# A gather loop of a graph network: one wait of GpSimd per superstep in place of four

## The chip, the cores and the metric

The kernel runs on one core of a Trainium2 chip. The metric is the device time of one execution in microseconds (us). The engines are TensorE (PE in the profile; its weight loads are PEld), VectorE (DVE), ScalarE (ACT), GpSimd (POOL, Pool in the text) and SyncE (SP), which here only sends transfers. Each runs its own list of instructions and meets the others at semaphores.

## The reference, cut to what matters

A graph of 12500 nodes with 64 features and 200000 edges, sorted by their target node `dst`, passes through two layers. The first is the one that matters here:

```
all_feat = concat([x[dst], x[src], edge_attr, u_per_node[dst]], axis=-1)
msg = relu(all_feat @ W1 + b1)
agg = segment_sum(msg, dst, num_segments=x.shape[0])
x = layernorm(x + relu(concat([x, agg, u_per_node]) @ W2 + b2))
```

The second layer is an attention over the same edges (a score, a softmax over the edges of a target, and a weighted sum), and ends in a layernorm too.

## The kernel before, in words

The kernel is one program with stages one after the other: inputs and the table of products `Btab` = x W1b, one row of 64 numbers per node; the first loop (`phase_layer0`); the nodes between the layers (`phase_mid`); the second loop (`phase_layer1`); the end. The change touches the first loop alone, though its helper `gathers` serves both.

*Tiles and slots.* The edges form 1563 tiles of 128. A tile whose targets lie in more than one block of 128 nodes is worked on once for each of these blocks; with these repeats there are 1664 slots, 8 of which (`O`) make a step: 208 steps (`SO`). The gathers go by supersteps of 8 tiles without repeats, 196 of them. A step thus uses tiles of its own superstep or of one up to 13 (`BEHIND`) earlier, the more so the further the loop has come.

*The ring.* Pool fetches, for each tile, the rows of `Btab` of its 128 source nodes with an indirect transfer into one of the 184 places of `ring` (23 supersteps, `RT`). This is line 453 in `gathers`. The loop needs these rows when VectorE fills `full` (line 853), which adds the ring's rows to TensorE's products of the edge features. A place may be overwritten when the step that last read it has filled: for gather j = 0 of superstep s Pool waits, at line 449, on `used`, which is S["full"] in the first loop, until the fill of step s - 10 has been made. At lines 451 and 452 it waits again, ahead of gathers j = 2, 4 and 6, on `summed`, which is S["acc"], until VectorE has made 2, 4 or 6 sums (line 846) of the tiles of step s - 11; VectorE makes those in step s - 9, behind the fill of that step. After its gather j = 3 Pool tells (`landed`) that the superstep before has arrived, once it has.

*One step s of the loop, by engine.* VectorE: one-hots of step s + 1 (line 830, float32, which waits for S["s"], the sums' products of an older step; and line 834, bf16); two reduces (line 873) of TensorE's products into `p_t`, which wait for S["m0"] and S["m1"]; loads of registers; the fill (line 853), which waits for `landed`; then, by turns, 8 sums of step s - 2 into the nodes' rows (line 846, on S["acc"]) and 8 additions to `p_t` (line 859). ScalarE: the relu of `p_t` into `msg` (line 632). TensorE: for step s + 1, behind the fill of s, 8 matmuls of line 719 and 4 of line 724 (float32, 2 passes each), which give S["m0"] after half of them and S["m1"] after all; then, behind the relu, the 8 matmuls of line 732 (float32, 16 passes) that give S["s"]. SP: the edge features of a later step (line 565) and, every 4 steps, the targets' rows `drow` (line 465).

Of the kernel before, what the change touches and what calls it, by code (L numbers as in the profile page):

```python
# [22 lines left out]
O = 8  # L23
# [6 lines left out]
RT = 23  # L30
# [45 lines left out]
CHUNKS = [(q, q + QC) for q in range(0, NQ, QC)]  # L76
# [353 lines left out]
def place(t):  # L430

    return t % RING


def gathers(e, A, ring, table, idx, s_g, landed, used, summed, free={}):

    tiles = lambda s: min(NT - s * O, O)


    def counted(s):  # L440
        e.wait_ge(s_g[s % len(s_g)], 16 * sum(tiles(i) for i in range(s % len(s_g), s + 1, len(s_g))))
        e.sem_inc(landed, 1)

    for t in range(NT):
        s, j = divmod(t, O)
        if s in free and j == 0:
            e.wait_ge(*free[s])
        if s >= RT and j == 0:
            e.wait_ge(used, s - RT + BEHIND + 1)

        if s >= RT and j in (2, 4, 6):
            e.wait_ge(summed, O * (s - RT + BEHIND - 1) + j)
        e.indirect_dma_start(out=ring[:, place(t), :], out_offset=None, in_=table[:, :],  # L453
                             in_offset=bass.IndirectOffsetOnAxis(ap=idx[:, t:t + 1], axis=0)).then_inc(s_g[s % len(s_g)], 16)
        if s and j == min(3, NT - s * O - 1):
            counted(s - 1)
    counted(TO - 1)
# [11 lines left out]
def phase_layer0(nc, A):  # L469
# [3 lines left out]
    with ExitStack() as ctx:  # L473
# [3 lines left out]
        ring = sb("ring0", [P, RING, D], F32)  # L477
# [3 lines left out]
        idx = A.idx0  # L481
# [5 lines left out]
        full = sb("full", [P, 2 * O, D], F32)  # L487

        XT0 = RING - NB
# [31 lines left out]
        S = {n: sem("l0_" + n) for n in names}  # L521
        s_g = [sem(f"l0_g{q}") for q in range(4)]
# [3 lines left out]
        T = {n: sem("t_" + n) for n in ("dve count before middle low high typ val sq sel tab d0 rows rowt rowi table dh dl lt yt ys "  # L526
                                        "drow typd ix a hi lo rem parts zero").split()}
# [44 lines left out]

        @block.gpsimd
        def _(e):
            gathers(e, A, ring, A.Btab, idx, s_g, S["landed"], S["full"], S["acc"], {XT0 // O: (T["a"], len(CHUNKS))})

        @block.scalar
        def _(e):
# [648 lines left out]
def phase_layer1(nc, A):  # L1227

    QO, QT, QV = 7, 5, 4
    with ExitStack() as ctx:  # L1230
# [43 lines left out]
        @block.gpsimd  # L1274
        def _(e):
            gathers(e, A, ring, A.Ztab, idx, s_g, S["landed"], S["s"], S["acc"])
# [425 lines left out]
```

## Time and profile before

| what | us |
|---|---|
| median of 3 runs | 5584.88 (5583.66 to 5586.26) |
| the profiled execution | 5585.71 |
| its span, from the first instruction to the last | 5584.0 |
| busy in it: PE, DVE, POOL, ACT | 3080.6, 2980.1, 3034.1, 1278.0 |
| first loop, from its first reduce to its last steps | about 178 to 2850 |

The rows below are of that one execution, in microseconds from the span's start. In a timeline row stand the start, the duration, the engine, the line, the operation, what it writes and reads, how many were merged, and in brackets the idle time of the engine before it with what ended it. "remote" is an end that the profile can't pin to an instruction, "issue" is time in which nothing was waited for that the profile shows. The ends of matmuls are modelled. A gather's row (DMA_INDIRECT) covers Pool's own work on it, not the transfer.

### The profile page before, as it was taken

The page shows a single profiled execution, that of the slowest core. Times are in us where ns is not written, and L with a number is a line of the kernel's source. Part 1 is how long each engine was busy: PE and PEld are TensorE (multiplying, and loading weights), DVE is VectorE, ACT ScalarE, POOL GpSimd, SP SyncE. Part 2 cuts the span into 40 slices and gives each one's busy share as a digit, 9 for nine tenths or more (in the row PEclk, how much of TensorE's full clock was granted, in tenths as well). Part 3 has the DMA queues.
Part 4 walks back from the last instruction along what each step waited for, and adds up shares of the span by engine and source line. Part 5 has one row for each costly group of instructions (what it writes and reads, how often), then busy time and mean ns, then how long its engine had stood idle before and what let it go on. Part 6 is the DMA issues. An engine that isn't in the chain of part 4 may idle for free. (4 is left out here: it accounts for less than half of the span.)

```text
span 5584.0 us, 71029 instructions
## 1 busy us (share of the span) xinstructions
PE 3080.6 (55%) x17849; PEld 2768.8 (50%) x17849; DVE 2980.1 (53%) x9486; ACT 1278.0 (23%) x4180; POOL 3034.1 (54%) x3265
## 2 busy tenths in 40 slices
PE   2265555455555555545784066555555656655576
PEld 1264444444444444444772055555555555555565
DVE  1265554455555555555773065555555555555567
ACT  0100000000000000000022044444444444444455
POOL 5525555555555555555215706666666666666631
PEclk5555555555555555555566555555555555555555
DMA  3211111111111111111125101111111111111111
GB/s 115 82 45 51 46 53 53 45 51 46 54 52 45 52 46 53 52 44 52 53 100 181 28 27 46 47 47 47 47 47 47 47 47 47 47 47 47 47 38 32
DMA packets 172540, 300.15 MB, mean 54 GB/s; under 512 B 71719, under 2 KB 78235, under 8 KB 158844
## 3 DMA queue, kind: packets, MB, share of 16 engines
q0 software_dynamic: 100032, 105.03, 9.8%
q1 hardware_dynamic: 70662, 188.25, 9.4%
q8 instruction: 173, 2.83, 0.2%
q10 hardware_dynamic: 1462, 2.30, 0.1%
q14 instruction: 211, 1.73, 0.1%
HBM read 260.36 MB, written 34.99 MB: 53 GB/s over the span
## 5 line engine op out<-in xcount | busy, mean ns | idle before, releaser
L453 POOL DMA_INDIRECT ring<-Btab,idx x1563 | 1486.5, 951 | 1214.7 <-DVE XA L846 610.3
L453 POOL DMA_INDIRECT ring<-Ztab,idx x1563 | 1479.9, 947 | 922.2 <-issue 400.0
L719 PE MATMUL p_m<-A,oht 128*128 x1664 | 438.3, 365 | 1061.8 <-DVE full L853 1023.5
L1344 PE MATMUL p_s<-ring,ohx 128*128 x3328 | 808.9, 420 | 191.2 <-issue 187.2
L732 PE MATMUL p_s<-msg,oh 128*128 128x64 f32 x3328 | 763.8, 418 | 178.2 <-issue 137.0
L1344 PEld LDWEIGHTS p_s<-ring,ohx 128*128 128x128 f32 x3328 | 738.8, 325 | 214.4 <-issue 214.1
L732 PEld LDWEIGHTS p_s<-msg,oh 128*128 128x128 f32 x3328 | 731.0, 329 | 204.8 <-issue 204.5
L873 DVE TENSOR_REDUCE p_t<-p_m 128x256 f32<-128x768 f32 x416 | 380.0, 958 | 817.4 <-remote 809.6
L719 PEld LDWEIGHTS p_m<-A,oht 128*128 128x128 bf16 x1664 | 237.6, 145 | 1153.8 <-issue 1109.8
L1402 DVE TENSOR_REDUCE mslot<-p_x 128x8 f32<-128x1024 f32 x208 | 254.7, 1225 | 896.8 <-remote 882.6
L632 ACT ACTIVATE msg<-p_t 128x512 f32<-128x512 f32 x208 | 124.2, 597 | 2552.7 <-issue 2161.9
L724 PE MATMUL p_m<-W1c,eaT 65*128 65x128 f32 x1664 | 572.6, 448 | 0.0
L1293 ACT ACTIVATE ohe<-oh,ev 128x128 f32<-128x128 bf16 x1664 | 505.2, 386 | 163.0 <-issue 104.1
L1432 DVE SCALAR_TENSOR_TENSOR XA<-XA,ff,p_s 128x65 f32 x1664 | 467.8, 281 | 130.4 <-issue 59.6
L1287 ACT ACTIVATE ohx<-oh,ex 128x128 f32<-128x128 bf16 x1664 | 508.9, 388 | 0.0
L724 PEld LDWEIGHTS p_m<-W1c,eaT 65*128 65x128 f32 x1664 | 455.8, 334 | 7.2 <-issue 0.4
L1318 PE MATMUL p_e<-S,oht 128*128 x1664 | 207.9, 189 | 399.3 <-issue 368.4
L830 DVE TENSOR_TENSOR oh<-p_i,dstl 128x1024 f32<-128x1024 f32 x208 | 253.2, 1217 | 314.9 <-remote 255.3
L1329 PE MATMUL p_x<-ident,ohe 128*128 128x128 f32 x1664 | 398.2, 418 | 1.8 <-issue 1.8
L859 DVE TENSOR_TENSOR p_t<-p_t,full 128x64 f32<-128x64 f32 x1664 | 386.0, 233 | 13.3 <-issue 7.5
L846 DVE TENSOR_TENSOR XA<-XA,p_s 128x64 f32 x1664 | 366.6, 220 | 37.6 <-issue 9.7
L1323 PE MATMUL p_e<-ring,ident_h 128*128 x1664 | 212.2, 185 | 285.5 <-issue 281.6
(211 smaller groups left out, 2716.4 us busy)
## 6 DMA issues: line engine op xcount, KB each, us to landing
drow<-drow_d SPq DMA_DIRECT2D x104, 1024.0 KB
eaT<-in_eaT_in SPq DMA_DIRECT2D x208, 128.0 KB
Ztab<-Z_stage SPq DMA_DIRECT2D x49, 536.0 KB, 5.1
ring<-Btab,idx POOLq DMA_INDIRECT x1563
ring<-Ztab,idx POOLq DMA_INDIRECT x1563
xTB<-in_xTB_in SPq DMA_DIRECT2D x7, 448.0 KB, 4.0
Btab<-B_stage SPq DMA_DIRECT2D x7, 448.0 KB, 6.0
ring<-in_xTA_in SPq DMA_DIRECT2D x7, 448.0 KB, 4.2
```

Of the source, the lines that this page charges most:

```text
L453: e.indirect_dma_start(out=ring[:, place(t), :], out_offset=None, in_=table[:, :], in_offset=bass.IndirectOffsetOnAxis(ap=idx[:, t:t + 1], ...
L719: e.matmul(parts(j), OHT[:, s % 2, j, :], A.A3[:, bass.ds(b, 1), :].rearrange("p a c -> p (a c)"), start=True, stop=True)
L724: last = e.matmul(own(j // 2), eaT[:, s % QE, j // 2, :], A.W1c2[:, :], start=True, stop=True)
L732: last = e.matmul(pS[r % 2][:, j, :], OH[:, r % QO, j, :], msg[:, r % 2, j, :], start=True, stop=True)
L846: e.tensor_tensor(out=acc, in0=acc, in1=pS[s % 2][:, j:j + 1, :], op=ALU.add).then_inc(S["acc"], 1)
L859: ins = e.tensor_tensor(out=pT[:, j:j + 1, :], in0=pT[:, j:j + 1, :], in1=full[:, bass.ds(t, 1), :], op=ALU.add)
L873: e.tensor_reduce(out=pT[:, h * H:(h + 1) * H, :], in_=half(h), axis=AXX, op=ALU.add).then_inc(T["dve"], 1)
L1287: ins = e.activation(OHx[:, o, j, :], OH[:, s % QO, j, :], ACT.Copy, scale=ex[:, o, j:j + 1])
L1293: ins = e.activation(OHe[:, s % 2, j, :], OH[:, s % QO, j, :], ACT.Relu, scale=ev[:, s % QV, j:j + 1])
L1329: last = e.transpose(pX[:, j, :], OHe[:, s % 2, j, :], A.ident[:, :])
L1344: last = e.matmul(pS[s % 2][h][:, j % 4, :], OHx[:, s % 2, j, :], ring[:, bass.ds(t, 1), 0:D + 1], start=True, stop=True)
L1432: e.scalar_tensor_tensor(out=acc, in0=acc, scalar=ff[:, s % QV, j:j + 1], in1=pS[s % 2][j // 4][:, j % 4:j % 4 + 1, :], op0=ALU.mult, op1= ...
```

## The change

In `gathers`, the waits ahead of gathers 2, 4 and 6 of a superstep are made only if a semaphore for them is given. The first loop gives none any more; the second loop still does. So in the first loop Pool waits once per superstep, at j = 0, for the fill of an older step.

```diff
-        if s >= RT and j in (2, 4, 6):
+        if summed is not None and s >= RT and j in (2, 4, 6):
             e.wait_ge(summed, O * (s - RT + BEHIND - 1) + j)
...
-            gathers(e, A, ring, A.Btab, idx, s_g, S["landed"], S["full"], S["acc"], {XT0 // O: (T["a"], len(CHUNKS))})
+            gathers(e, A, ring, A.Btab, idx, s_g, S["landed"], S["full"], None, {XT0 // O: (T["a"], len(CHUNKS))})
```

## Rows read from the trace of the kernel before

**Rows 1.** The page: the span, and the costliest group of instructions.

```profile
span 5584.0 us, 71029 instructions
...
L453 POOL DMA_INDIRECT ring<-Btab,idx x1563 | 1486.5, 951 | 1214.7 <-DVE XA L846 610.3
```

**Rows 2.** Windows: length, then each engine's busy time (x instructions), PEclk, DMA share, GB/s.

```profile
core 0: us, PE busy (x) PEld busy (x) DVE busy (x) ACT busy (x) POOL busy (x), PEclk, DMA share, GB/s
300.00:390.00 90.00, 75.50 (x352) 69.60 (x352) 76.67 (x234) 6.57 (x11) 0.00 (x0) 0.50 0.12 40
600.00:1000.00 400.00, 209.31 (x960) 190.88 (x959) 207.53 (x630) 17.92 (x30) 225.97 (x239) 0.50 0.18 51
...
2710.00:2800.00 90.00, 87.77 (x411) 80.95 (x409) 87.06 (x270) 7.76 (x13) 0.00 (x0) 0.50 0.16 55
```

**Rows 3.** Timeline of one cycle, 1502 to 1529 us, chosen instructions.

```profile
1502.23 0.69 DVE L853 TENSOR_TENSOR full<-p_m,ring 128x512 f32 x1
...
1513.05 1.23 DVE L830 TENSOR_TENSOR oh<-p_i,dstl 128x1024 f32<-128x1024 f32 x1 [6.81 <-remote]
...
1515.52 0.94 POOL L453 DMA_INDIRECT ring<-Btab,idx  x1 [0.30 <-issue]
1519.48 1.83 DVE L873 TENSOR_REDUCE p_t<-p_m 128x256 f32<-128x768 f32 x2 [4.76 <-remote]
1521.99 0.69 DVE L853 TENSOR_TENSOR full<-p_m,ring 128x512 f32 x1 [0.69 <-issue]
...
1523.50 0.94 POOL L453 DMA_INDIRECT ring<-Btab,idx  x1 [7.04 <-DVE XA L846]
...
1525.63 0.69 PE L724 MATMUL p_m<-W1c,eaT 65*128 65x128 f32 x2
...
1527.16 1.82 DVE L873 TENSOR_REDUCE p_t<-p_m 128x256 f32<-128x768 f32 x2
...
1528.89 0.68 DVE L853 TENSOR_TENSOR full<-p_m,ring 128x512 f32 x1
```

**Rows 4.** Line 453 from 300 to 2710 us: count, idle time by what ended it.

```profile
L453 POOL DMA_INDIRECT ring<-Btab,idx x1379: 942/947/1175, 390.2 to 2703.3; - x197
its engine sat idle before it (us, times) until:
  DVE XA L846: 610.3, 87
...
  DVE full L853: 91.4, 1
```

**Rows 5.** Timeline, 387 to 402 us: the one start of Pool on a fill.

```profile
389.21 0.69 DVE L853 TENSOR_TENSOR full<-p_m,ring 128x512 f32 x1 [0.28 <-issue]
...
390.18 0.94 POOL L453 DMA_INDIRECT ring<-Btab,idx  x1 [91.36 <-DVE full L853]
...
397.61 0.95 POOL L453 DMA_INDIRECT ring<-Btab,idx  x1 [5.24 <-DVE XA L846]
```

**Rows 6.** Timeline of the prologue, 170 to 330 us, where Pool gathers without a stop.

```profile
178.68 0.69 PE L724 MATMUL p_m<-W1c,eaT 65*128 65x128 f32 x2
...
180.53 0.97 DVE L873 TENSOR_REDUCE p_t<-p_m 128x256 f32<-128x768 f32 x1 [1.76 <-PE p_m L724]
...
186.03 0.69 PE L724 MATMUL p_m<-W1c,eaT 65*128 65x128 f32 x2
...
196.80 0.97 DVE L873 TENSOR_REDUCE p_t<-p_m 128x256 f32<-128x768 f32 x1 [10.85 <-remote]
...
217.71 0.97 DVE L873 TENSOR_REDUCE p_t<-p_m 128x256 f32<-128x768 f32 x1 [19.95 <-remote]
...
229.59 0.26 PE L732 MATMUL p_s<-msg,oh 128*128 128x64 f32 x1 [2.54 <-issue]
```

**Rows 7.** Timeline, 602 to 612 us: the cycle whose one-hots came latest.

```profile
603.89 0.94 POOL L453 DMA_INDIRECT ring<-Btab,idx  x1 [0.30 <-issue]
605.62 1.22 DVE L830 TENSOR_TENSOR oh<-p_i,dstl 128x1024 f32<-128x1024 f32 x1 [11.01 <-remote]
...
607.89 1.83 DVE L873 TENSOR_REDUCE p_t<-p_m 128x256 f32<-128x768 f32 x2 [0.65 <-remote]
```

## The prediction

> **What bounds the kernel now.** I began with the page: Pool is busy for about half of the span in gathers that take 0.95 us each and come 1.25 us apart at the closest, and the gathers of the first loop are the costliest group of all, with 1214.7 us of idle time ahead of them, half of it put down to a sum of VectorE, line 846 [rows 1]. So the first loop is where to look. The table of windows then shows the point of this case. Where Pool has nothing to do (300 to 390 us, and 2710 to 2800 us), VectorE and TensorE are busy for 80 to 97% of the time. Where Pool gathers, both drop to about half [rows 2]. In steps: the fill of line 853 comes every 7 us in the first kind of stretch, and there the loop is bound by VectorE's own work.
>
> The timeline of one cycle shows how the half comes about [rows 3]. Fills start at 1502.23, 1521.99 and 1528.89: a step of 19.8 us and one of 6.9 us, by turns. In the long step VectorE stands still ahead of the reduce of line 873, which waits for m0 and m1, TensorE's word that the products of the step are there. The records of those matmuls end long before; the word comes late. What it comes after is Pool: the last gather of a burst ends at 1515.52 + 0.94 = 1516.46 and the reduce starts at 1519.48, 3.02 us later. In another cycle the same distance is 607.89 - 604.83 = 3.06 us [rows 7]. The prologue shows the same with Pool working without a break: the first step's reduces start close to the end of their matmuls (178.68 + 0.69 = 179.37, and the reduce at 180.53), the next step's at 196.80 and only at 217.71, and matmuls of line 732 then come one by one, 2.5 us apart [rows 6]. I read from this: **while Pool gathers, TensorE gets about one step's work through and then crawls; 3 us after Pool stops, all is released.**
>
> And Pool stops because of its waits. A cycle is a ring of causes: Pool's burst (16 gathers), 3.02 us, reduces and register loads 2.51 us (1519.48 to 1521.99), fill 0.69 us (to 1522.68), then two sums of line 846, and Pool starts at 1523.50, 0.82 us after the end of the fill [rows 3]. During the burst one quick step passes. The view of line 453 says how often: 87 stops on a sum, 610.3 us, and one stop on a fill [rows 4]. One of the 87 is the short one of 5.24 us at the beginning [rows 5]; the other 86 are (610.3 - 5.2) / 86 = 7.04 us each. Bursts are 16 long all through: 1379 gathers = 2 + 86 x 16 + 1. A cycle takes (2703.3 - 397.6) / 86 = 26.81 us [rows 4, 5].
>
> **The change, part by part.** It takes out three waits of Pool per superstep (ahead of gathers j = 2, 4 and 6) and adds nothing; no data is moved and VectorE still counts S["acc"] for its own order. As instructions the waits are free. What matters is which wait ends Pool's stop. In code, gather j = 0 of superstep g waits for the fill of step g - 10, and j = 2 waits for two sums that VectorE makes in step g - 9, just after its fill. So today j = 0 and 1 of a superstep are sent at the end of a burst, the stop is at j = 2, and it ends on a sum. After the change the stop is at j = 0 and ends on the fill itself.
>
> What a start on a fill costs, the trace has once: a fill ends at 389.21 + 0.69 = 389.90, Pool starts at 390.18, 0.28 us later [rows 5]. Today it is 0.82 us. **The gain of one stop is 0.82 - 0.28 = 0.54 us.**
>
> How many stops follow from the same count: after the first 184 gathers there are 1379 = 86 x 16 + 3. A burst starts at a fill (step i), sends superstep g (10 us), finds the fill of the quick step i + 1 done (6.9 us after the first: 1528.89 - 1521.99 [rows 3]), sends g + 1, and stops, since step i + 2 is the one that can't end while Pool works. So a burst stays 16 long, there are 86 long steps as before, and the one that is now a burst of 2 is merged into the first. The phase begins one step earlier, and one more quick step stands at the end; these cancel.
>
> The sum, against the profiled execution's span of 5584.0 us (its time 5585.7; the median of the runs, 5584.9, is 0.8 below that): 86 x 0.54 = 46.4 us. All of it lies on the path, since the cycle is a ring with no slack in it but the quick step. 5584.9 - 46.4 = **5538.5 us**, -0.83%. A cycle goes from 26.81 to 26.27 us, a stop from 7.04 to 6.50.
>
> Next to be late, where the wait goes: nothing in the ring; its members keep their lengths. The cover that must hold is that of the quick step i + 1: its matmuls of lines 719 and 724 now run wholly beside gathers, where they had 0.54 us more of a quiet Pool. Their last record ends at 1525.63 + 0.69 = 1526.32, 3.64 us after the fill; the second reduce needs them at 1527.16 + 0.87 = 1528.03, 5.35 us after it [rows 3] (0.87 is half of the two reduces of 1.82, less their overlap). Slack 1.7 us. In the prologue, under an unbroken Pool, the like block was 180.53 - 179.37 = 1.2 us late [rows 6]. That fits, so I take a cost of zero. The other end: work of TensorE that passes now in the quiet 0.54 us (2 or 3 matmuls) is passed at the crawl of about 2 us each, so that S["s"], for which the one-hots of line 830 wait in the long step, comes up to 5 us later. Today that start lies anywhere: at 1513.05, 3.4 us ahead of the burst's end [rows 3], and at the latest, at 605.62, 0.8 us behind it, with no harm to the reduce [rows 7]. Harm begins at 3.02 - 1.6 = 1.4 us behind the end (1.6 us from the one-hots' start to the reduce). By the starts of line 830 in the 86 cycles, 9 would pass that point if all moved by 5 us, and each would cost at most the 1.6 us by which they could push the reduce: 9 x 1.6 = 14 us. Bounds of this term: 0 and +14 us. On the other side, Pool might start as the fill's count arrives with less delay than 0.28: at most 0.06 us or so (the difference between the quickest and the slowest start seen is 0.01), 86 x 0.06 = 5 us.
>
> By the trace, Pool and TensorE hinder one another (half the busy share when Pool gathers [rows 2]). The Trainium skill says otherwise: its page "SBUF — State Buffer", section "SBUF: two separate sides", has only the port pair that VectorE and GpSimd share as a point of contention, and TensorE never waiting on anyone there. If that held for all that TensorE does here, the long step's 13 us would be the loop's own and not Pool's, and an earlier start of Pool would bring nothing. That would be the outcome of rival 1, 5584.9 us; rows 2 and 6 speak against the page.
>
> **Rivals.**
> 1. *The long step has its own length*: what ends it is tied to TensorE's own start, and not to the end of the burst (or Pool is held in place of the removed wait by another, such as the landing of its gathers ahead of the fourth gather). For it: in a cycle whose parts all have fixed lengths, a clock that starts at the fill fits as well as one that starts at the burst's end. Against: the prologue, where the two reduces of one step lay 217.71 - 196.80 = 21 us apart while Pool went on, in place of less than 1 us [rows 3, 6]. Time 5584.9, no change.
> 2. *Slower: the quick step is lost.* If the matmuls of step i + 1 no longer pass beside the gathers, each superstep becomes a burst of its own. A step is then 8 x 0.95 + 7 x 0.30 = 9.7 us of burst, 3.02, 2.51, 0.69 and 0.28: 16.2 us in place of 26.81 / 2 = 13.4, so 172 x 2.8 = 481 us more: 6066 us. It decides when the fill of step i + 1 comes later than Pool's ninth gather, 10.3 us behind the fill, in place of 6.9: the second reduce may be 3.4 us late, and m1 1.7 + 3.4 = 5.1 us. The prologue's first block was 1.2 us late and the second, twice as many matmuls in, 217.71 - 186.72 = 31 us [rows 6]; so the edge lies between one block and two, and we are at one.
> 3. *Longer bursts*: if the third step passed as well, 24 gathers would share one stop: (24 x 1.25 + 6.2) / 3 = 12.1 us a step, 172 x 1.3 = 224 us less, 5361 us. Nothing in 86 cycles hints at it.
>
> **How the numbers follow.** My forecast, with its late one-hots between 0 and 14 us: 0.83. Rival 1: 0.07. Rival 2: 0.06, and 0.01 for a slowing that I don't see. Rival 3: 0.03. The range takes the forecast's case alone, 5538.5 - 5 to 5538.5 + 14, with 3 us at the upper and 1 us at the lower end for the spread of runs (5583.66 to 5586.26): 5532 to 5556. A difference within 0.2%, 11 us, is about what a measurement can't tell from none: faster 0.86, same 0.07, slower 0.07.
>
> **What would show it.** Right: 86 stops of Pool in the view of line 453, now ended by "DVE full L853", 6.5 us each and none by line 846; Pool starting 0.28 us behind the fill; the reduce of the long step still 3.0 us behind the last gather; 26.3 us a cycle; steps of 7 us and 19.3 us by turns; the second loop unchanged. Rival 1: stops of 7.04 us as before, with the reduce 3.6 us behind the burst. Rival 2: about 172 stops. Late one-hots: line 830 in long steps starting more than 1.4 us behind the burst's end. Wrong from the ground up would be the reading that Pool's silence frees TensorE: then the reduce would not keep its distance to the last gather.

## The result, and the profile after

The changed kernel takes 5596.7 us (5593.5 to 5599.8, 16 runs) where the kernel before takes 5585.35 us (5583.6 to 5587.0, 16 runs): 11.3 us more, ratio 1.002, 95% interval 1.0013 to 1.0028. 5538.5 us were forecast. Its profiled execution took 5594.65 us, its span is 5592.9 us against 5584.0.

First the line of the gathers from 300 to 2710 us, with what ended Pool's idle time; it answers [rows 4].

```profile
L453 POOL DMA_INDIRECT ring<-Btab,idx x1379: 938/944/1039, 389.6 to 2708.9; - x197
its engine sat idle before it (us, times) until:
  DVE full L853: 715.9, 87
```

There are 86 stops behind the first one (91.2 us), all ended by the fill, as forecast, and there is none on line 846 any more. But a stop lasts (715.9 - 91.2) / 86 = 7.26 us, not 6.50, and before 7.04. The last burst has 3 gathers and so starts at 2708.9 - 2 x 1.25 = 2706.4; a cycle takes (2706.4 - 389.6) / 86 = 26.94 us against 26.81. 86 x 0.13 = 11 us: the whole difference lies in the cycles of the first loop.

Now one cycle of the changed kernel, chosen rows of its timeline, for [rows 3]:

```profile
1492.82 0.68 DVE L853 TENSOR_TENSOR full<-p_m,ring 128x512 f32 x1
...
1493.77 0.94 POOL L453 DMA_INDIRECT ring<-Btab,idx  x1 [7.37 <-DVE full L853]
...
1497.32 3.65 PE L732 MATMUL p_s<-msg,oh 128*128 128x64 f32 x16 [0.18 <-ACT msg L632]
...
1497.98 1.82 DVE L873 TENSOR_REDUCE p_t<-p_m 128x256 f32<-128x768 f32 x2
...
1499.71 0.68 DVE L853 TENSOR_TENSOR full<-p_m,ring 128x512 f32 x1
...
1504.23 1.94 PE L732 MATMUL p_s<-msg,oh 128*128 128x64 f32 x8
...
1512.29 0.26 PE L732 MATMUL p_s<-msg,oh 128*128 128x64 f32 x1 [1.84 <-issue]
1512.49 0.94 POOL L453 DMA_INDIRECT ring<-Btab,idx  x1 [0.30 <-issue]
1514.40 0.27 PE L732 MATMUL p_s<-msg,oh 128*128 128x64 f32 x1 [1.85 <-issue]
1516.49 0.92 PE L732 MATMUL p_s<-msg,oh 128*128 128x64 f32 x4 [1.82 <-issue]
1516.56 1.22 DVE L830 TENSOR_TENSOR oh<-p_i,dstl 128x1024 f32<-128x1024 f32 x1 [13.10 <-remote]
...
1518.09 1.82 DVE L873 TENSOR_REDUCE p_t<-p_m 128x256 f32<-128x768 f32 x2
1519.82 0.68 DVE L853 TENSOR_TENSOR full<-p_m,ring 128x512 f32 x1
...
1520.77 0.94 POOL L453 DMA_INDIRECT ring<-Btab,idx  x1 [7.34 <-DVE full L853]
```

The reader is to see four things. Pool starts 0.27 us behind the fill (1493.50 to 1493.77). The quick step is there. The burst ends at 1512.49 + 0.94 = 1513.43. And then it isn't the reduce that starts 3 us later but the one-hots of line 830, at 1516.56, 3.13 us behind; the reduce has to queue behind them and starts at 1518.09, 4.66 us behind. Against the cycle of before: the reduce comes 1.64 us later; from the reduce to the fill it takes 1.73 us in place of 2.51, 0.78 less (the reduces now queue behind the one-hots, and the 0.69 us of idle time ahead of the fill is gone; by the program's order that is where the register loads lie, though no row shows them); Pool starts 0.54 us earlier. Together +0.32 us, and 7.04 + 0.32 = 7.36 us, against 7.34 in the last row. The median of the 86 stops is 7.36 us too; 6 stops of 6.4 to 6.6 us and 17 of 7.0 to 7.2 us bring the mean to 7.26.

The sum of VectorE's idle time ahead of line 830 says how general this is. Before, then after, each from 300 to 2710 us:

```profile
L830 DVE TENSOR_TENSOR oh<-p_i,dstl x185: 1211/1215/1225, 315.2 to 2705.5; 128x1024 f32<-128x1024 f32 x185
its engine sat idle before it (us, times) until:
  remote: 213.7, 52
```

```profile
L830 DVE TENSOR_TENSOR oh<-p_i,dstl x184: 1214/1215/1226, 314.7 to 2709.1; 128x1024 f32<-128x1024 f32 x184
its engine sat idle before it (us, times) until:
  remote: 1060.6, 85
```

By the starts of line 830, in 83 of the 86 cycles of the changed kernel they lie more than 1.4 us behind the burst's end (80 of them 2.8 to 3.4 us, median 3.14 us); in the kernel before none did. The mean of the 86 distances from the burst's end to the reduce goes from 2.99 to 4.54 us.

### The profile page after: what moved, and what is told of

It is laid out like the page before. It is cut to its first block and busy times, and to the rows that moved or that the text cites. A ratio compares the mean times of both kernels' runs of the same rounds, so it can differ in the third digit from the quotient of the medians.

```text
span 5592.9 us, 71029 instructions
## 1 busy us (share of the span) xinstructions
PE 3097.5 (55%) x17849; PEld 2790.8 (50%) x17849; DVE 2966.6 (53%) x9486; ACT 1277.6 (23%) x4180; POOL 3023.3 (54%) x3265
## 3 DMA queue, kind: packets, MB, share of 16 engines
q14 instruction: 211, 1.73, 0.1%
## 5 line engine op out<-in xcount | busy, mean ns | idle before, releaser
L453 POOL DMA_INDIRECT ring<-Btab,idx x1563 | 1477.8, 945 | 1229.0 <-DVE full L853 715.9
L732 PE MATMUL p_s<-msg,oh 128*128 128x64 f32 x3328 | 790.9, 404 | 857.8 <-issue 828.6
L732 PEld LDWEIGHTS p_s<-msg,oh 128*128 128x128 f32 x3328 | 758.4, 324 | 906.9 <-issue 906.6
```

The costliest lines, as they stand in the source:

```text
L732: last = e.matmul(pS[r % 2][:, j, :], OH[:, r % QO, j, :], msg[:, r % 2, j, :], start=True, stop=True)
```

## Experiments

The runs went to several chips, and these are of two kinds. On some the kernel before takes 5584 to 5625 us, as here; on others 4193 to 4200 us. Each kernel is compared with the kernel before on its own chip.

**Theory 1**: S["s"], for which line 830 waits, comes late in the changed kernel and is alone to blame. **Theory 2**: Pool's earlier start leaves TensorE more to catch up with, so the release itself comes later, the reduce's too.

### The changed kernel, again

> The changed kernel itself beside the kernel before. Where the kernel before takes 5585 us, both theories expect 5597 us and one-hots 3.1 us behind the burst. Where it takes 4199 us, as in the four runs ahead of this one (Pool there gathers without stops and TensorE isn't held up), Pool sets the pace of the first loop, 1379 gathers x 1.25 us, and the removed waits end nothing: no change within 0.1%.

5632.5 us against 5625.4 us, ratio 1.0012 (1.0001 to 1.0023): the small loss appears on a second chip, though only just clear of none, and all 86 one-hots lie 3.0 to 3.5 us behind the burst.

### A fourth buffer of one-hots

```diff
-    QE, QO = 2, 3
+    QE, QO = 2, 4
```

In the changed kernel:

> The changed kernel with four buffers of one-hots, once more, for a chip on which the kernel before takes about 5600 us. Theory 1 (the late S["s"] alone costs): one-hots right behind the quick step, the reduce 3.0 us behind the last gather, a stop of Pool 6.5 us, a cycle 26.2 to 26.3 us, and 40 to 55 us less than the kernel before, ratio 0.990 to 0.993. Theory 2 (the release itself comes later): the reduce stays 4.7 us behind, ratio 1.001 to 1.002. Where the kernel before takes 4199 us: no change.

In the kernel before:

> The kernel before with four buffers of one-hots. Theory 1: its one-hots were early enough already, so no change beyond 3 us, ratio 0.9995 to 1.0005. If it gains as much as the changed kernel does, the buffer is worth something for a reason of its own.

Changed kernel with it: 5553.3 us against 5586.5 us, ratio 0.9941 (0.9924 to 0.9958), 33 us less. Kernel before with it: 5585.35 us, ratio 1.000 (0.999 to 1.0009). The buffer is worth 33 + 11 = 44 us to the changed kernel, if it loses 11 us on this chip as on the first (it wasn't run on this one), and nothing to the kernel before. The line of the gathers, the line of the one-hots, and one cycle of the changed kernel with four buffers:

```profile
L453 POOL DMA_INDIRECT ring<-Btab,idx x1379: 942/947/1176, 391.2 to 2667.4; - x197
```

```profile
L830 DVE TENSOR_TENSOR oh<-p_i,dstl x190: 1212/1215/1225, 316.3 to 2709.9; 128x1024 f32<-128x1024 f32 x190
its engine sat idle before it (us, times) until:
  issue: 0.2, 1
```

```profile
1511.32 1.22 DVE L830 TENSOR_TENSOR oh<-p_i,dstl 128x1024 f32<-128x1024 f32 x1
...
1519.90 0.95 POOL L453 DMA_INDIRECT ring<-Btab,idx  x1 [0.30 <-issue]
1523.92 1.83 DVE L873 TENSOR_REDUCE p_t<-p_m 128x256 f32<-128x768 f32 x2 [11.00 <-remote]
```

The one-hots never wait, and the reduce is back at 1523.92 - 1520.85 = 3.07 us behind the burst (the mean of the 86 is 3.20 us, the median 3.26 us). A cycle takes (2667.4 - 2.5 - 391.2) / 86 = 26.44 us. So theory 1 holds for most of it: what the change adds to the mean distance falls from 1.55 us (4.54 - 2.99) to 0.21 us (3.20 - 2.99). These 0.21 us are the part for theory 2. A stop is then 0.54 - 0.21 = 0.33 us shorter than in the kernel before, 28 us in 86 cycles, and a burst takes 19.73 in place of 19.78 us, another 4 us less: 32 of the 33 us measured.

### Pool's start moved back, its stop left at gather 0

```diff
+        if later is not None and s >= RT and j == 0:
+            e.wait_ge(later, O * (s - RT + BEHIND - 2) + 2)
```

(`later` is S["acc"], in the first loop alone.)

> The changed kernel with one wait more at gather j = 0, for two sums behind the fill, so that Pool starts 0.82 us behind the fill as before, and stops at j = 0. Theory 1a (what counts is how much of the quick step's TensorE work passes before Pool starts): as before, one-hots of the long step 9 to 20 us after the start of the burst, ratio 1.000. Theory 1b (what counts is at which gather Pool stops): one-hots 3.1 us behind the burst, and 46 us more than the changed kernel, ratio 1.010.

5620.8 us against 5586.5 us, ratio 1.0063 (1.0046 to 1.0079). The start came out later than meant: with a second wait at the same gather, for the same two sums, Pool starts 1.30 us behind the fill, not 0.82, 0.48 us later. One cycle (lines are 2 further down in this kernel):

```profile
1498.64 0.94 POOL L455 DMA_INDIRECT ring<-Btab,idx  x1 [0.30 <-issue]
1500.44 0.97 DVE L875 TENSOR_REDUCE p_t<-p_m 128x256 f32<-128x768 f32 x1 [10.08 <-remote]
1502.54 0.97 DVE L875 TENSOR_REDUCE p_t<-p_m 128x256 f32<-128x768 f32 x1 [1.13 <-remote]
1505.02 0.69 DVE L855 TENSOR_TENSOR full<-p_m,ring 128x512 f32 x1 [1.52 <-issue]
...
1507.02 0.94 POOL L455 DMA_INDIRECT ring<-Btab,idx  x1 [7.43 <-DVE XA L848]
...
1511.92 0.68 DVE L855 TENSOR_TENSOR full<-p_m,ring 128x512 f32 x1
...
1515.56 1.22 DVE L832 TENSOR_TENSOR oh<-p_i,dstl 128x1024 f32<-128x1024 f32 x1
```

The one-hots start right behind the quick step, 8.5 to 9.5 us into the burst, in 75 of 85 cycles, though Pool stops at gather 0. So a stop at gather 0 doesn't by itself make the one-hots late (theory 1b of the expectation falls), and the start behind the fill is what is left. In 22 of the 85 cycles m0 now comes before the release (the first reduce at 1500.44, 0.86 us behind the burst, the second at 1502.54, 2.96 us behind), so TensorE gets further the later Pool starts. The extra 0.48 us of the start times 86 are 41 us, near the 34 measured. Three starts and what became of the one-hots, counted from the burst's end; the last column has how many of the long step's 16 matmuls of line 732 are recorded in a row before they begin to come one by one:

| Pool's start behind the fill | one-hots of the long step | matmuls in a row |
|---|---|---|
| 0.27 us (changed kernel) | 2.8 to 3.4 us behind it in 80 of 86, median 3.1 | 6 to 14, median 8 |
| 0.82 us (kernel before) | between 10.7 us ahead of it and 0.8 us behind it, median 7.7 ahead | 12 to 16, all 16 in 48 of 86 |
| 1.30 us (this kernel) | median 10.9 us ahead of it, at the latest 5.3 us ahead | all 16 in 80 of 85 |

### Half the gathers

```diff
+    sent = lambda s, j: table is not A.Btab or s < RT or j % 2 == 0
...
+        if sent(s, j):
             e.indirect_dma_start(out=ring[:, place(t), :], out_offset=None, in_=table[:, :],
```

> The changed kernel with every second gather of the first loop left out from superstep 23 on, the waits kept (the places keep old rows, so the node features that come out are other ones). If the end of Pool's burst frees TensorE, the second half of a burst of 8 gathers starts at the quick step's fill, 6.9 us behind the first fill, ends at 11.9 us, and the long step's reduce follows at 15 to 16.5 us and its fill at 18 to 19 us: 19 us a cycle in place of 27, 690 us less in the first loop. If the long step has its own length (rival 1 of the prediction), the cycle stays at 26 to 27 us. If 4 gathers are too few to hold TensorE at all, 14 us a cycle, 1120 us less.

4522 us against 5586.5 us (one run; the kernel leaves gathers out, so its results are other ones). Windows of it, then of the kernel's own gather line:

```profile
core 0: us, PE busy (x) PEld busy (x) DVE busy (x) ACT busy (x) POOL busy (x), PEclk, DMA share, GB/s
600.00:1000.00 400.00, 384.35 (x1782) 352.56 (x1781) 378.84 (x1165) 33.43 (x56) 210.06 (x223) 0.50 0.26 73
```

```profile
L455 POOL DMA_INDIRECT ring<-Btab,idx x690: 938/944/1131, 389.3 to 1634.3; - x173
its engine sat idle before it (us, times) until:
  DVE full L855: 511.9, 167
```

TensorE and VectorE are busy for 95% in place of 52% [rows 2], while Pool is busy nearly as much as before (210 of 400 us against 226). A step takes (1634.3 - 389.3) / 172 = 7.2 us, and from 600 to 1500 us VectorE waits ahead of the reduces once, for 0.7 us (kernel before: 34 times, 293.1 us). Nothing on TensorE's or VectorE's lists was changed, so the long step has no length of its own: rival 1 of the prediction is out, and Pool's share of busy time isn't what holds TensorE. What about the gathers it is, this kernel doesn't say: each group of 4 is followed by a stop of 511.9 / 167 = 3.07 us, so a rate, the length of a group and a silence of 3 us would all fit. The transfers are halved with the gathers, so it doesn't say either whether it is Pool's own work or the transfers that count.

### Rests on Pool, and chips of the other kind

All these have the changed waits and four buffers. Behind gathers 3 and 7 (a_rest_2, a_rest_4) or behind each (the others) Pool sets a scratch tile of its own to zero:

```diff
+        if rest is not None and j in (0, 1, 2, 3, 4, 5, 6, 7):
+            for _ in range(1):
+                if rest[2]:
+                    e.wait_ge(rest[1], rest[2])
+                e.memset(rest[0][:, :], 0.0).then_inc(rest[1], 1)
+                rest[2] += 1
```

> The changed kernel with four buffers of one-hots, and with Pool busy for itself (two memsets of 128 x 512 numbers, about 0.5 us each by the 0.2 us of one of 128 x 128 in the trace) behind its fourth and eighth gather of each superstep of the first loop: 4 gathers, about 1.2 us without one, 4 gathers. If the gathers alone hold TensorE, by the rate at which they come, a short rest may let it through: then no long steps, the first loop goes at Pool's pace, 8 x 1.25 + 2 x 1.2 = 12.4 us a step in place of 13.4, and the time is 150 to 200 us below the kernel before (ratio 0.965 to 0.975). If TensorE is held until the full 3 us behind a last gather have passed, the rests only make the burst longer: 2 x 2.4 us more per cycle, 5553 + 86 x 4.8 = 5966 us, ratio 1.07. Where the kernel before takes 4199 us, Pool sets the pace already and each rest is added: 196 x 2.4 = 470 us more.

> The same with four memsets at each place, about 2.4 us of rest, what the kernel with half its gathers had between its groups of 4 (2.3 us), where TensorE kept up. Let through: 8 x 1.25 + 2 x 2.4 = 14.8 us a step, against 13.4 in the kernel before; the prologue's 184 gathers hold nothing either, 60 to 80 us less there: ratio 1.02 to 1.04, and no long steps in the trace. Held all the same: 5553 + 86 x 9.6 = 6380 us.

> The same as a_rest_2 with one memset of 128 x 256 numbers (about 0.3 us) behind every gather. If what holds TensorE is the rate of gathers over some microseconds, it is worth the same here as in groups: 8 x 1.6 = 12.8 us a step when let through, ratio 0.975 to 0.985. If it is the length of an unbroken group that counts (4 pass, 8 don't), this one passes too, for no group is longer than 1. If only a silence near 3 us lets it through, cycles of 16 gathers as before, each 5 us longer: ratio 1.07.

These three met a chip of 4200 us, and there took 4617 us (ratio 1.099, 1.097 to 1.101), 5074 us (1.208, 1.205 to 1.210) and 4522 us (1.076, 1.074 to 1.078). Sent again as a_rest_2_r, a_rest_4_r and a_rest_each_r they met another of that kind, with 4607, 5063 and 4512 us against 4193, the same ratios:

> As for a_rest_2, on a chip where the kernel before takes about 5600 us. Where Pool doesn't hold TensorE this kernel takes 4617 us. If 4 gathers in a row pass beside TensorE and a rest of about 1 us clears the way: no long steps, between 4617 and 4800 us, ratio 0.83 to 0.86 when the second loop is as quick as there, and, since that loop has no rests and keeps its pace of before, rather 0.96 to 0.975. If a silence of 3 us is needed: ratio 1.05 to 1.07, bursts of 16.

> As for a_rest_4, on such a chip. 4 gathers in 7 us held nothing in the kernel with half its gathers, so in all theories but the one of 3 us of silence: no long steps, Pool's pace, about 14.7 us a step, ratio 1.00 to 1.04. With 3 us of silence needed: above 1.1.

> As for a_rest_each, on such a chip: if the length of an unbroken group decides, no long steps and Pool's pace, ratio 0.95 to 0.97. If the rate decides (a gather per 1.25 us holds, one per 1.75 us doesn't), this one at a gather per 1.5 us lies between: long steps, but shorter or fewer. If the silence decides: bursts of 16, ratio 1.03 to 1.07.

On such a chip each rest is simply added, since Pool sets the pace. That is also why the first four runs of the study, which met one, told nothing of the change: the changed kernel with four buffers 4197.9 us, the kernel before with four 4200.1, the delayed start 4200.3, and the kernel before without its waits at gathers 4 and 6 4199.7, all against 4199.4 us.

> The changed kernel with four buffers of one-hots in place of three, so that line 830 in the long step waits for an S["s"] that is one step older. Theory 1 (the late S["s"] alone costs: in the changed kernel the one-hots start 3.13 us behind the burst and push the reduce from 3.02 to 4.67 us behind it): the one-hots start right behind the quick step, the reduce is back at 3.0 us behind the last gather, a stop of Pool is 6.5 us, a cycle 26.2 us, the time about 5597 - 86 x 0.85 = 5524 to 5540 us. Theory 2 (Pool's earlier start leaves TensorE with more to catch up, so the release itself comes later): the reduce stays 4.7 us behind the last gather and the time at 5597 us.

> The kernel before with four buffers of one-hots. Its reduce was 3.02 us behind the burst whether its one-hots came 10.7 us ahead of the burst's end or 0.8 us behind it. Theory 1: no change, 5585 us within 3 us, the reduce still 3.0 us behind. Theory 2 says nothing else. If this kernel gains as much as the changed one does from the fourth buffer, the buffer is worth something for a reason of its own and theory 1 falls.

> The changed kernel with one more wait at gather j = 0, for two sums of the same step's fill, so that Pool starts 0.82 us behind the fill as before, but still stops at j = 0 and once per superstep. Theory 1a (what counts is how much of the quick step's TensorE work passes before Pool starts): as before, one-hots of the long step spread over 9 to 20 us after the start of the burst, reduce 3.0 us behind the burst, 5585 us. Theory 1b (what counts is at which gather Pool stops, with the word on landed transfers and its waits at other places in the burst): as in the changed kernel, one-hots 3.1 us behind the burst, and with the start 0.54 us later about 5597 + 46 = 5643 us.

> The kernel before with the waits of the first loop at gathers 4 and 6 taken out and that at gather 2 kept. In the trace of before only the wait at gather 2 ends a stop, so both theories expect the same cycles as before: bursts of 16, Pool starting 0.82 us behind the fill, 5585 us. If instead it is like the changed kernel, the waits in mid-superstep do something that no stop shows.

What such a chip looks like, by a_qo4's gather line and one window:

```profile
L453 POOL DMA_INDIRECT ring<-Btab,idx x1435: 943/947/1177, 199.2 to 1995.8; - x180
```

```profile
600.00:1000.00 400.00, 295.26 (x1348) 266.14 (x1347) 288.14 (x882) 25.08 (x42) 302.73 (x320) 0.50 0.26 67
```

Gathers take the same 947 ns and come (1995.8 - 199.2) / 1434 = 1.25 us apart without a single long stop, and beside them the other engines do a step in 9.5 us on average (fills 20 to 190 of the loop); from 600 to 1500 us VectorE never waits ahead of a reduce. TensorE isn't held. So what holds TensorE is a matter of the chip as well as of Pool. On b_j2 the question it was made for stays open, for it never ran on a chip of the other kind; nor did the rests behind gathers 3 and 7.

The one that settled the rests ran alone and met a chip of the 5584 us kind:

> As for a_rest_each_r, on a chip where the kernel before takes about 5600 us. If TensorE is let through: no long steps, 8 x 1.55 = 12.4 us a step at Pool's pace against 13.4, ratio 0.95 to 0.97. If the rate decides and 1.55 us is still too quick: long steps, though fewer or shorter. If only a silence decides: bursts of 16, ratio 1.03 to 1.07. Where the kernel before takes 4200 us: 1.076 as there.

5206.8 us against 5583.8 us, ratio 0.9325 (0.9298 to 0.9352), **377 us less** (2 runs), the fastest of this study on such a chip that makes all its gathers. 33 us of it the four buffers gave alone (5553.3 us, same chip); the rests gave the other 5553.3 - 5206.8 = 346 us, with the 3 us between the two reference times left in. A window of it, its gather line, a piece of its timeline, and its reduces from 600 to 1500 us (line 881 here is line 873 of the others):

```profile
600.00:1000.00 400.00, 228.29 (x1039) 205.13 (x1039) 230.72 (x690) 19.11 (x32) 354.35 (x550) 0.50 0.21 55
```

```profile
L453 POOL DMA_INDIRECT ring<-Btab,idx x1381: 952/953/1214, 300.3 to 2319.0; - x198
its engine sat idle before it (us, times) until:
  issue: 222.0, 1369
  DVE full L861: 14.4, 12
```

```profile
1002.91 0.95 POOL L453 DMA_INDIRECT ring<-Btab,idx  x1 [0.16 <-issue]
1003.86 0.33 POOL L459 MEMSET rest<- 128x256 f32 x1
1004.35 0.95 POOL L453 DMA_INDIRECT ring<-Btab,idx  x1 [0.16 <-issue]
```

```profile
L881 DVE TENSOR_REDUCE p_t<-p_m x149: 946/967/967, 608.9 to 1497.7; 128x256 f32<-128x768 f32 x149
its engine sat idle before it (us, times) until:
  remote: 246.2, 124
```

Pool hardly stops at all (12 times, 14.4 us), a gather comes every 1.44 us, and TensorE nearly keeps up with Pool: a step takes 11.9 us on average (fills 20 to 190 of the loop) in place of 13.4, and the last gather of the loop is sent at 2319.0 in place of 2703.3 us. TensorE is still held, though: VectorE waits ahead of 124 of 149 reduces, 246.2 us in all, where the kernel before waits 293.1 us in 34 waits, the kernel with half its gathers 0.7 us, and the same kernel on a chip of 4200 us not at all. So with gathers 1.44 us apart the 13 us by which every second step was longer are gone, and in their place stand waits of about 2 us ahead of most reduces. The prediction's reading, a silence of 3 us as the price of release, was too narrow: here words of finished matmuls come while Pool goes on. Whether it is the rate of the gathers that counts, the length of an unbroken group, or the mere presence of another instruction between two gathers, this run doesn't separate.

Two more kernels were to fill in a point between and to try the second loop; they met a chip of 4193 us again:

> As a_rest_each, with a memset of 128 x 32 numbers behind each gather of the first loop: about 0.1 us of work and 1.25 us or a little more from gather to gather. On a chip with 5580 us before: if the rate decides, TensorE is held longer than in a_rest_each_s, time between 5207 and 5553 us. If the mere presence of another instruction between gathers is enough, 8 x 1.3 = 10.4 us a step, about 5050 us. On a chip with 4200 us before: 4200 to 4260 us.

> As a_rest_each, with the rests in the second loop too. On a chip with 5580 us before: if the rate decides, the second loop (about 12 us a step, with TensorE's matmuls of lines 1318 and 1323 coming 1.25 us apart beside the gathers) goes at Pool's pace of 8 x 1.44 = 11.6 us or near it, 0 to 100 us less than 5207 us. If the second loop is held by something else, each step is 8 x 0.19 = 1.5 us longer, 300 us more than 5207 us. On a chip with 4200 us before: 4830 us.

a_rest_both took 4842 us there (ratio 1.155, 1.151 to 1.158), each rest added. a_rest_short took 4204 us once and 8005 us once, the latter at a mean granted clock of 0.18 in place of 0.52, and nothing is read from that. What either does on a chip of the 5584 us kind is open.

## Why the prediction was wrong, point by point

- *Where to look, and how the cycle hangs together*: right. Bursts of 16, 86 of them, a quick and a long step by turns, the release behind Pool's last gather. The half of the gathers confirmed that Pool's gathers hold TensorE. The 3 us of silence as the price of release was too narrow a reading: with rests word of finished matmuls came between gathers.
- *The stop ends on the fill, 0.28 us behind it, 0.54 us earlier*: right, 0.27 us, and no stop of another kind took its place.
- *"The other end" of the cover, the one-hots*: **the step that failed, by its size.** The mechanism was named: less of TensorE's work passes before Pool starts, S["s"] comes later, line 830 pushes the reduce. But I moved the starts by 5 us at most (2 or 3 matmuls at 2 us) and so found 9 cycles past the point of harm, at up to 1.6 us, 14 us in all. The median start of the one-hots moved by 10.9 us, from 7.7 us ahead of the burst's end to 3.1 us behind it; 83 of 86 cycles were past the point, and the reduce came 1.55 us later on average, 133 us ahead of what is given back. That these late one-hots are the cause, the fourth buffer shows: without their wait the changed kernel is 33 us quicker than the kernel before. How far back TensorE falls can be seen at line 732: in the kernel before, 14 of the 16 matmuls of the long step in the cycle of [rows 3] were recorded before they began to come one by one,

```profile
1499.77 3.65 PE L732 MATMUL p_s<-msg,oh 128*128 128x64 f32 x16
...
1507.01 3.01 PE L732 MATMUL p_s<-msg,oh 128*128 128x64 f32 x13 [0.40 <-ACT msg L632]
...
1510.20 0.27 PE L732 MATMUL p_s<-msg,oh 128*128 128x64 f32 x1 [0.18 <-issue]
```

  and after the change 8 (the row at 1504.23 above): six matmuls that come 2.1 us apart, not two or three. That is a sign of TensorE's delay and not the delay of S["s"] itself. With three buffers, the one-hots of step s + 1 wait for the products of step s - 2, and these are the 16 matmuls of line 732 that came a step earlier, recorded at 1499.77 before and at 1497.32 after, long before their word arrives. With four buffers the row of matmuls breaks off as early (median 8 of 16), and it costs next to nothing. Why the word of the older products comes only with the release in nearly every cycle, instead of being spread over 11 us as before, the runs don't say: that the small shift of 0.54 us sets TensorE back so far is shown, by what mechanism is open.
- *What it gives back*: not seen. When the one-hots come first, the way from the reduce to the fill is shorter, on average by 0.76 us (2.53 to 1.77 us). Per cycle 1.55 - 0.76 - 0.55 = +0.24 us of stop (7.04 to 7.26 us by the view of line 453), less the burst's own 0.1 us (19.78 to 19.68 us), is within rounding of the 0.13 us of a cycle and the +11 us. The forecast's term for the earlier start, 46 us, was right. That the loss is only 11 us is luck and no merit of the sum: 133 us later reduces stand against 47 us of the start, 65 us of the shorter way to the fill and 9 us of shorter bursts, and the prediction had the last two at nothing.
- *"Nothing in the ring is late next"*: wrong for the same reason. I had argued the cover of the reduce (m1, slack 1.7 us, which held: the quick steps kept their 6.9 us) and treated S["s"] as a bound, though the rows had it anywhere from 10.7 us ahead of the burst's end to 0.8 us behind it. A wait whose end scatters over 11 us, when the reduce of the same step repeats within 0.9 us (2.68 to 3.54 us behind the burst), should have been given a case of its own.
- *Rivals*: 2 (one burst per superstep, 6066 us) and 3 (24 gathers) did not happen. Rival 1 is out by the half of the gathers; theory 2's later release, 0.21 us with four buffers, is no case of it.
- *The skill's rule*: the page "SBUF — State Buffer" of the Trainium skill, section "SBUF: two separate sides", has TensorE wait on no one on the side of the engines. Read as widely as the prediction did, for all that TensorE does, the trace differs on chips where the kernel takes 5584 us (TensorE busy 52% beside gathers 1.25 us apart and 95% with half of them), and the measurement decides; on those of 4200 us nothing here contradicts it. The page speaks of the ports of SBUF alone, and whether TensorE is held there or elsewhere no row shows.

## What to carry to other kernels

When a wait is made to end earlier in a cycle that repeats, look for the waits whose end scatters in the trace of before: a small shift can move all its cases at once (here 0.54 us moved 83 of 86), so price it at its full cost times all cycles as a case of its own. Give the buffer that such a wait guards one place more before moving anything (here about 44 us for 4 KB per partition, and nothing where it wasn't late). And where an engine that issues transfers runs at its peak rate beside others that stand still meanwhile, try it a little slower: 0.2 us more per gather gave about 345 us here. But try it on the chip that will run it: on the other kind of chip the same rests cost 7.6%.

## What the runs showed of the hardware that was not expected

- The same kernel takes 5584 to 5625 us on some chips and 4193 to 4200 us on others, with the same durations of single instructions (a gather 947 ns on both, the mean granted clock 0.52 on both). What differs in the traces is whether TensorE passes beside Pool's gathers: from 600 to 1500 us VectorE waits 293.1 us ahead of its reduces on the former (kernel before) and not at all on the latter (changed kernel with four buffers). Each chip that ran more than one kernel stayed of its kind; what makes the kind is open.
- On the former, gathers 1.25 us apart let TensorE's matmuls of line 732 through at one per 2.1 us after about one step; 1.44 us apart (0.33 us of memset between) they hold it less (246.2 us of waits ahead of the reduces, spread over 124), and the kernel is 6.7% faster, four buffers included. What TensorE and Pool share isn't shown by any row, nor whether it is Pool's own work, the transfers of the gathers or another queue that holds TensorE.
- A second semaphore wait ahead of the same gather put its start back by 0.48 us (1.30 in place of 0.82 us behind the fill). Waits that were fulfilled already cost nothing: in the kernel before, the gaps ahead of gathers 4 and 6, which have a wait, are 0.30 us like all others.
